# A feed-forward pass in straight-line code: second product in rows, wide sums on DVE, last scaling on ACT

## The chip, the cores and the metric

One core of a Trainium2 chip runs the kernel. The metric is the device time of one execution in microseconds (us). The engines go by short names: PE or TensorE (matrix products; PEld are its weight loads), DVE (VectorE), ACT (ScalarE), POOL (GpSimd) and SP (SyncE, which issues most of the transfers). All numbers are fp32. An fp32 product is two matmul instructions, and the trace counts instructions.

## What is computed

The reference runs a relational graph layer twice, then a transformer block with attention along the edges, on 50,000 nodes of 128 features and 25,000 edges, with a layer norm and a residual around each. The change lies in the end of the transformer block, which treats each node by itself:

```python
x = residual + att                      # att = agg @ Wo + bo
residual = x
h = _layer_norm(x, g2, b2)
ffn = gelu(h @ W1 + bf1) @ W2 + bf2     # 128 -> 512 -> 128
block = residual + ffn
...
x = _layernorm(x + block)               # the kernel's output
```

The kernel has g2 and b2 folded into W1 and bf1. The attention stage leaves two rows per node in the DRAM tensor `x_rows`: X1, the block's input x, and X2, the residual with the attention's output but without `bo`. The output is the layer norm of X1 + X2 + bo + ffn.

## The kernel before

The kernel is a series of programs, one after the other with a barrier between: `prepare`, `dense`, two of `layer`, `attention`, `softmax`, `weighted`, and last `ffn`. The nodes go through `ffn` in 98 groups of 512 (GT = 4 tiles of 128 nodes; a group lies in SBUF as 128 partitions by 4 nodes by 2 by 128 features, 512 KB). Each engine walks the same series of steps, in order, and in step n does its several pieces of work for groups n, n-1, n-2 and so on; semaphores that count groups tie the engines together.

`over_tiles` (line 54) writes the steps: the first 16 as straight code, then a hardware loop (`Fori`) with 16 steps unrolled in its body, then the rest. `Turn.ago(lag)` gives the group that is `lag` steps back. In the loop the semaphore values come from registers. `gate` (line 166) adds an increment of a semaphore of its own ahead of waiting instructions on SP, POOL and DVE.

What a group g goes through, with its lag:

- SP loads both rows of 512 nodes into `xs[g % 16]` (lag 0, line 1671), and stores `res` (lag 14, line 1661).
- POOL adds `bo` to X2 (lag 0, line 1698), adds X2 to X1 (lag 1, line 1705), and computes the inverse roots `rstd` (lag 3) and `rstd2` (lag 12) by two instructions of 4 columns each, `var` (line 1687) and a power of -0.5 (line 1690).
- DVE takes mean and variance of X2 (bn_stats line 1784, bn_aggr line 1798, lag 2), scales it to `normed` (lag 4), adds the second product to X1 (lag 11, line 1778), takes mean and variance of that (lines 1791 and 1810), and scales it to `res` (lag 13). Both scalings are in the helper at line 1769, four instructions of 128 columns.
- PE turns `normed` so that features lie on partitions (lag 5, line 1723, `p_n`), makes the first product in four chunks of 128 hidden features (lag 7, line 1717, `p_f`), the second, summed over the four chunks (lag 8, line 1730, `p_y`), and turns that back into rows of nodes (lag 10, line 1737, `p_r`).
- ACT copies the turned rows to `nT` (lag 6, line 1754), makes the gelus (lag 7, line 1761), and copies the second product with the bias `bf2` per partition to `yT` (lag 9, line 1749).

The second product has the weights stationary and the activations moving, and so comes out with features on partitions:

```python
mm = e.matmul(p_y[:], w_2[:, ch, :], g_T[:, s, ch, :], start=(ch == 0), stop=(ch == FCH - 1))
...
e.activation(yT[:, s, :], p_y[:], ACT.Identity, bias=bf2[:]).then_inc(yT_ready, 1)
...
mm = e.transpose(p_r[s][:, a * D:(a + 1) * D], yT[:, s, a * P:(a + 1) * P], ident[:])
```

## Time and profile before

| | |
|---|---|
| median of 3 executions | 2708.08 us (2704.77 to 2711.64) |
| the profiled execution | 2707.31 us, its span 2705.6 us |
| busy over the span | PE 79%, PEld 57%, DVE 74%, ACT 45%, POOL 61% |
| `ffn` | from the first load's issue at 1910.73 us to the end |
| busy time of the two products of `ffn` | `p_f` 354.1 us, `p_y` 352.8 us |

The shares are means over stages with different limits; only the stretch from 1910 us on bears on the change. Matmuls overlap one another in the trace, so the duration of a group of matmuls says less than the distance between starts. "Idle before" is an engine's waiting time just ahead of an instruction, put down to whatever ended last. POOL's durations are rough.

### The profile page before, as it was taken

The page shows a single profiled execution, that of the slowest core. Times are in us where ns is not written, and L with a number is a line of the kernel's source. Part 1 is how long each engine was busy: PE and PEld are TensorE (multiplying, and loading weights), DVE is VectorE, ACT ScalarE, POOL GpSimd, SP SyncE. Part 2 cuts the span into 40 slices and gives each one's busy share as a digit, 9 for nine tenths or more (in the row PEclk, how much of TensorE's full clock was granted, in tenths as well). Part 3 has the DMA queues.
Part 4 walks back from the last instruction along what each step waited for, and adds up shares of the span by engine and source line. Part 5 has one row for each costly group of instructions (what it writes and reads, how often), then busy time and mean ns, then how long its engine had stood idle before and what let it go on. Part 6 is the DMA issues. An engine that isn't in the chain of part 4 may idle for free. (4 is left out here: it accounts for less than half of the span.)

```text
span 2705.6 us, 46439 instructions
## 1 busy us (share of the span) xinstructions
PE 2142.7 (79%) x11670; PEld 1533.3 (57%) x11670; DVE 1996.6 (74%) x7853; ACT 1204.7 (45%) x2725; POOL 1663.1 (61%) x1791
## 2 busy tenths in 40 slices
PE   3777776747776777599999228885499999999997
PEld 3555555537776777568778226664244444444443
DVE  4888888856665777688888766664467877887775
ACT  2888888832222454456666200000244444444443
POOL 2777777757775776275552007777666666666662
PEclk9889899879888998899999659887799999999999
DMA  3788788766657999644452024664322333333231
GB/s 87 224 244 241 238 240 241 235 186 179 183 165 221 297 300 278 205 127 124 122 126 80 17 71 147 184 194 140 116 78 99 104 105 99 100 105 105 94 98 50
DMA packets 378850, 422.87 MB, mean 156 GB/s; under 512 B 54814, under 2 KB 263274, under 8 KB 378614
## 3 DMA queue, kind: packets, MB, share of 16 engines
q1 hardware_dynamic: 334774, 337.16, 39.9%
q0 software_dynamic: 40768, 82.23, 11.7%
q8 instruction: 84, 1.38, 0.2%
q14 instruction: 152, 1.25, 0.1%
q10 hardware_dynamic: 3072, 0.86, 0.1%
HBM read 273.58 MB, written 179.87 MB: 168 GB/s over the span
## 5 line engine op out<-in xcount | busy, mean ns | idle before, releaser
L1717 PE MATMUL p_f<-nT,w 128*128 128x512 f32 x784 | 354.1, 594 | 0.0
L1730 PE MATMUL p_y<-g_T,w 128*128 128x512 f32 x784 | 352.8, 593 | 0.8 <-ACT yT L1749 0.8
L1120 POOL DMA_INDIRECT x_src<-x_rows,idx x196 | 185.7, 947 | 166.1 <-DVE normed L1287 73.0
L1761 ACT ACTIVATE g_T<-p_f,bf 128x512 f32<-128x512 f32 x392 | 261.5, 688 | 34.6 <-PE p_f L1717 34.4
L1525 POOL DMA_INDIRECT x_rows<-xv,idx x196 | 211.5, 1079 | 85.9 <-issue 52.1
L1698 POOL TENSOR_TENSOR xs<-xs,bo_rows 128x512 f32<-128x512 f32 x98 | 129.0, 1317 | 212.4 <-DMA xs<-x_rows 197.2
L575 POOL DMA_INDIRECT x_dst<-in_x_dram,idx x196 | 195.2, 996 | 101.7 <-issue 101.7
L911 POOL DMA_INDIRECT h_src<-h_table,idx x196 | 191.1, 975 | 87.4 <-issue 56.7
L911 POOL DMA_INDIRECT h_src<-in_x_dram,idx x196 | 190.4, 972 | 75.8 <-issue 58.5
L1690 POOL TENSOR_TENSOR rstd<-var,minus_half 128x4 f32<-128x4 f32 x196 | 206.8, 1055 | 35.9 <-POOL var L1687 35.8
L1749 ACT ACTIVATE yT<-p_y,bf 128x512 f32<-128x512 f32 x98 | 67.4, 688 | 358.9 <-PE p_r L1737 352.5
L579 POOL DMA_INDIRECT e_h<-in_L_gnn_rel_embed_dram,idx x196 | 189.1, 965 | 59.8 <-issue 59.8
L1717 PEld LDWEIGHTS p_f<-nT,w 128*128 128x128 f32 x784 | 142.2, 191 | 142.4 <-issue 119.7
L1730 PEld LDWEIGHTS p_y<-g_T,w 128*128 128x128 f32 x784 | 141.5, 190 | 142.6 <-issue 141.6
L976 ACT ACTIVATE low<-p_h 128x512 f32<-128x512 f32 x98 | 58.5, 597 | 342.9 <-PE p_h L949 342.9
L1754 ACT ACTIVATE nT<-p_n 128x512 f32<-128x512 f32 x98 | 57.7, 589 | 329.9 <-PE p_n L1723 329.9
L1778 DVE TENSOR_TENSOR xs<-p_r,xs 128x512 f32<-128x512 f32 x98 | 67.8, 692 | 181.9 <-PE p_r L1737 181.9
L1769 DVE TENSOR_SCALAR normed<-xs,mv,rstd 128x128 f32<-128x128 f32 x392 | 168.1, 492 | 1.9 <-POOL rstd L1690 1.3
L1769 DVE TENSOR_SCALAR res<-xs,mv,rstd 128x128 f32<-128x128 f32 x392 | 167.4, 488 | 0.8 <-POOL rstd L1690 0.8
L652 PE MATMUL p_r<-ident,h1T 128*128 128x128 f32 x392 | 69.6, 305 | 119.6 <-ACT h_rows L689 119.4
L948 PE MATMUL p_h<-w_r,accT 128*128 128x128 f32 x784 | 160.9, 289 | 0.0
L949 PE MATMUL p_h<-w_sl,ownT 128*128 128x128 f32 x784 | 159.2, 286 | 0.0
(297 smaller groups left out, 5886.8 us busy)
## 6 DMA issues: line engine op xcount, KB each, us to landing
xs<-x_rows SPq DMA_DIRECT2D x98, 512.0 KB, 3.7
x_in<-in_x_dram SPq DMA_DIRECT2D x98, 256.0 KB, 3.7
h_table<-h_rows SPq DMA_DIRECT2D x98, 256.0 KB, 4.0
x_rows<-x_in SPq DMA_DIRECT2D x98, 256.0 KB, 4.5
out_dram<-res SPq DMA_DIRECT2D x98, 256.0 KB, 2.0
x_rows<-x_rows SPq DMA_DIRECT2D x50, 500.0 KB
rows<-edge_rows SPq DMA_DIRECT2D x147, 128.0 KB, 4.5
edge_x<-x_dst SPq DMA_DIRECT2D x98, 128.0 KB
```

The source lines that it names most:

```text
L575: e.indirect_dma_start(out=x_dst[:, m % PN, j, :], out_offset=None, in_=x, in_offset=bass.IndirectOffsetOnAxis(ap=idx[:, DST, 2 * m + j:2 ...
L579: e.indirect_dma_start(out=e_h[:, t, :], out_offset=None, in_=L0_gnn_rel_embed, in_offset=bass.IndirectOffsetOnAxis(ap=idx[:, TYPE, t:t + ...
L911: e.indirect_dma_start(out=h_src[:, g % HN, j, :], out_offset=None, in_=(x, h1_table)[l], in_offset=bass.IndirectOffsetOnAxis(ap=idx[:, (S ...
L948: e.matmul(p_h[g % 2][:, at], accT[:, g % 2, at], w_r[l][:], start=True, stop=False)
L949: mm = e.matmul(p_h[g % 2][:, at], ownT[:, g % 2, at], w_sl[l][:], start=False, stop=True)
L1120: e.indirect_dma_start(out=x_src[:, k % SN, j, :], out_offset=None, in_=x_rows, in_offset=bass.IndirectOffsetOnAxis(ap=idx[:, X_SRC, t:t + ...
L1525: e.indirect_dma_start(out=both_table.rearrange("n a d -> n (a d)"), in_=xv[:, g % VN, j, :, :].rearrange("p a d -> p (a d)"), in_offset=None,
L1690: e.tensor_tensor(rstd[:, s, :], var[:, s, :], minus_half[:], ALU.pow).then_inc(rstd_ready, 1)
L1717: e.matmul(p_f[ch][:], w_1[:, ch * P:(ch + 1) * P], nT[:, s, :], start=True, stop=True)\
L1730: mm = e.matmul(p_y[:], w_2[:, ch, :], g_T[:, s, ch, :], start=(ch == 0), stop=(ch == FCH - 1))
L1761: e.activation(g_T[:, s, ch, :], p_f[ch][:], ACT.Gelu, bias=bf1[:, ch:ch + 1]).then_inc(gelu_ready, 1)
L1769: ins = e.tensor_scalar(into[:, a * D:(a + 1) * D], rows_in[:, a, :], mean[:, a, 0:1], scale[:, a:a + 1], ALU.subtract, ALU.mult)
```

## The change

The change rewrites `ffn` and nothing else, except that `bf2` is now loaded as a row repeated on all 128 partitions (`bf2_rows`).

- All steps are straight code; `Turn`, `over_tiles`, `gate` and their semaphores are gone, and every wait is for a constant.
- The second product has the activations stationary: for each of the four tiles of nodes and each chunk, `g_T` (128 x 128) is the stationary operand and 128 columns of `w_2` move. It comes out in rows of nodes, in one of two PSUM buffers. The copy `yT` and the turn back `p_r` are gone; the PSUM they held is used for a second `p_n` and `p_y`.
- The bias `bf2`, which `yT` added, is now added to X1 in rows by DVE.
- DVE makes all wide sums: X2 + bo, X1 + X2, + bf2, + second product. POOL keeps `var` and the power.
- The last scaling moves from DVE to ACT, four instructions of 128 columns with scale `rstd2` and bias `shift2` = -mean x rstd2, which DVE computes (4 columns). They stand between the gelus.
- `xs` has 14 buffers instead of 16, `res` 4 instead of 16. Lags: DVE's first work 2 steps behind the load, the store 13.

The core of the diff (line 1624 of the new file is the wait before the store, and so on in order):

```diff
-        bf2 = sb("bf2", [P, 1])
+        bf2_rows = sb("bf2_rows", [P, D])
...
-                    e.dma_start(bf2[:], L1_gnn_bf2.rearrange("(p a) -> p a", a=1)).then_inc(loaded, 16)
+                    e.dma_start(bf2_rows[:], L1_gnn_bf2.partition_broadcast(P)).then_inc(loaded, 16)
...
+            XN, RN = 14, 4
...
-                yT = sb("yT", [P, 2, GROUP], F32, c)
...
-                p_n = ps("p_n", c)
...
-                p_y = ps("p_y", c)
-                p_r = [ps(f"p_r{s}", c) for s in range(2)]
...
+                shift2 = sb("shift2", [P, 2, GT], F32, c)
+                p_n = [ps(f"p_n{s}", c) for s in range(2)]
...
+                p_y = [ps(f"p_y{s}", c) for s in range(2)]
...
+                A = 2
+                STEPS = NG + A + 12
...
+                        if at_step(n, A + 11):
+                            g = n - A - 11
+                            if g == NG - 1:
+                                e.wait_ge(stored[(g - 1) % RN], 16 * ((g - 1) // RN + 1))
+                            e.wait_ge(res_ready, g + 1)
+                            e.dma_start(rows(out, g).rearrange("(p a) d -> p (a d)", a=GT), res[:, g % RN, :, :].rearrange("p a d -> p (a d)"))\
+                                .then_inc(stored[g % RN], 16)
+                        if at_step(n, 0):
+                            g = n
+                            wait(e, res_ready, g - XN + 1)
+                            wait(e, both_ready, g - XN + 1)
+                            wait(e, normed_ready, g - XN + 1)
+                            e.dma_start(xs[:, g % XN, :, :, :].rearrange("p a w d -> p (a w d)"),
+                                        rows(both_table, g).rearrange("(p a) w d -> p (a w d)", a=GT)).then_inc(xs_loaded[g % XN], 16)
...
+                    for n in range(STEPS):
+                        if at_step(n, A + 1):
+                            g = n - A - 1
+                            e.wait_ge(mv_ready, g + 1)
+                            e.tensor_scalar(var[:, g % 2, :], mv[:, g % 4, :, 1], EPS, None, ALU.add).then_inc(var_ready, 1)
+                            e.wait_ge(var_ready, g + 1)
+                            wait(e, normed_ready, g - 1)
+                            e.tensor_tensor(rstd[:, g % 2, :], var[:, g % 2, :], minus_half[:], ALU.pow).then_inc(rstd_ready, 1)
+                        if at_step(n, A + 8):
+                            g = n - A - 8
+                            e.wait_ge(mv2_ready, g + 1)
+                            e.tensor_scalar(var2[:, g % 2, :], mv2[:, g % 4, :, 1], EPS, None, ALU.add).then_inc(var2_ready, 1)
+                            e.wait_ge(var2_ready, g + 1)
+                            wait(e, res_ready, g - 1)
+                            e.tensor_tensor(rstd2[:, g % 2, :], var2[:, g % 2, :], minus_half[:], ALU.pow).then_inc(rstd2_ready, 1)
...
+                    for n in range(STEPS):
+                        if at_step(n, A + 5):
+                            g = n - A - 5
+                            e.wait_ge(nT_ready, g + 1)
+                            for ch in range(FCH):
+                                wait(e, gelu_ready, FCH * (g - 1) + ch + 1)
+                                e.matmul(p_f[ch][:], w_1[:, ch * P:(ch + 1) * P], nT[:, g % 2, :], start=True, stop=True).then_inc(f_prod, 1)
+                        if at_step(n, A + 6):
+                            g = n - A - 6
+                            e.wait_ge(gelu_ready, FCH * (g + 1))
+                            wait(e, sum_ready, g - 1)
+                            for a in range(GT):
+                                for ch in range(FCH):
+                                    mm = e.matmul(p_y[g % 2][:, a * D:(a + 1) * D], g_T[:, g % 2, ch, a * P:(a + 1) * P], w_2[:, ch, :],
+                                                  start=(ch == 0), stop=(ch == FCH - 1))
+                            mm.then_inc(y_prod, 1)
+                        if at_step(n, A + 3):
+                            g = n - A - 3
+                            e.wait_ge(normed_ready, g + 1)
+                            wait(e, nT_ready, g - 1)
+                            for a in range(GT):
+                                mm = e.transpose(p_n[g % 2][:, a * P:(a + 1) * P], normed[:, g % 2, a, :], ident[:])
+                            mm.then_inc(n_turned, 1)
...
-                            e.activation(yT[:, s, :], p_y[:], ACT.Identity, bias=bf2[:]).then_inc(yT_ready, 1)
...
+                    for n in range(STEPS):
+                        if at_step(n, A + 4):
+                            g = n - A - 4
+                            e.wait_ge(n_turned, g + 1)
+                            wait(e, f_prod, FCH * (g - 1))
+                            e.activation(nT[:, g % 2, :], p_n[g % 2][:], ACT.Copy).then_inc(nT_ready, 1)
+                        for ch in range(FCH):
+                            if at_step(n, A + 5):
+                                g = n - A - 5
+                                e.wait_ge(f_prod, FCH * g + ch + 1)
+                                if ch == 0:
+                                    wait(e, y_prod, g - 1)
+                                e.activation(g_T[:, g % 2, ch, :], p_f[ch][:], ACT.Gelu, bias=bf1[:, ch:ch + 1]).then_inc(gelu_ready, 1)
+                            if at_step(n, A + 10):
+                                g = n - A - 10
+                                if ch == 0:
+                                    e.wait_ge(shift2_ready, g + 1)
+                                    wait(e, stored[g % RN], 16 * (g // RN))
+                                ins = e.activation(res[:, g % RN, ch, :], xs[:, g % XN, ch, X1, :], ACT.Identity,
+                                                   scale=rstd2[:, g % 2, ch:ch + 1], bias=shift2[:, g % 2, ch:ch + 1])
+                                if ch == GT - 1:
+                                    ins.then_inc(res_ready, 1)
...
+                    for n in range(STEPS):
+                        if at_step(n, A + 7):
+                            g = n - A - 7
+                            x1 = xs[:, g % XN, :, X1, :]
+                            e.wait_ge(y_prod, g + 1)
+                            e.wait_ge(both_ready, g + 1)
+                            e.tensor_tensor(x1, p_y[g % 2][:].rearrange("p (a d) -> p a d", a=GT), x1, ALU.add).then_inc(sum_ready, 1)
+                        if at_step(n, A):
+                            g = n - A
+                            x2 = xs[:, g % XN, :, X2, :]
+                            e.wait_ge(xs_loaded[g % XN], 16 * (g // XN + 1))
+                            e.tensor_tensor(x2, x2, over_rows(bo_rows), ALU.add).then_inc(x2_ready, 1)
+                        if at_step(n, A + 7):
+                            g = n - A - 7
+                            e.wait_ge(sum_ready, g + 1)
+                            wait(e, mv2_ready, g - 1)
+                            for a in range(GT):
+                                ins = e.bn_stats(stats2[:, g % 2, a, :], xs[:, g % XN, a, X1, :])
+                            ins.then_inc(stats2_ready, 1)
...
+                        if at_step(n, A + 2):
+                            g = n - A - 2
+                            e.wait_ge(rstd_ready, g + 1)
+                            wait(e, n_turned, g - 1)
+                            for a in range(GT):
+                                ins = e.tensor_scalar(normed[:, g % 2, a, :], xs[:, g % XN, a, X2, :], mv[:, g % 4, a, 0:1],
+                                                      rstd[:, g % 2, a:a + 1], ALU.subtract, ALU.mult)
+                            ins.then_inc(normed_ready, 1)
+                        if at_step(n, A + 9):
+                            g = n - A - 9
+                            e.wait_ge(rstd2_ready, g + 1)
+                            wait(e, res_ready, g - 1)
+                            e.scalar_tensor_tensor(out=shift2[:, g % 2, :], in0=mv2[:, g % 4, :, 0], scalar=-1.0, in1=rstd2[:, g % 2, :],
+                                                   op0=ALU.mult, op1=ALU.mult).then_inc(shift2_ready, 1)
...
+                        if at_step(n, A + 3):
+                            g = n - A - 3
+                            x1 = xs[:, g % XN, :, X1, :]
+                            e.tensor_tensor(x1, x1, xs[:, g % XN, :, X2, :], ALU.add).then_inc(pair_ready, 1)
+                        if at_step(n, A + 4):
+                            g = n - A - 4
+                            x1 = xs[:, g % XN, :, X1, :]
+                            e.wait_ge(pair_ready, g + 1)
+                            e.tensor_tensor(x1, x1, over_rows(bf2_rows), ALU.add).then_inc(both_ready, 1)
```

On PE, one step of the middle of the pass and the start of the next, before. `p_f` is the first product, `p_n` the turn of the normed rows, `p_y` the second product, `p_r` the turn back.

```order
L1717 MATMUL p_f_1<-nT,w_1 128x512 x4
L1723 MATMUL p_n<-ident,normed 128x128 x4
L1730 MATMUL p_y<-g_T,w_1 128x512 x4
L1737 MATMUL p_r_1<-ident,yT 128x128 x4
L1717 MATMUL p_f_1<-nT,w_1 128x512 x4
```

And now:

```order
L1663 MATMUL p_f_1<-nT,w_1 128x512 x4
L1670 MATMUL p_y_1<-w_1,g_T 128x128 x16
L1678 MATMUL p_n_1<-ident,normed 128x128 x4
L1663 MATMUL p_f_1<-nT,w_1 128x512 x4
L1670 MATMUL p_y_1<-w_1,g_T 128x128 x16
```

The second product has four times as many instructions of a quarter of the columns and stands right behind the first; the turn back is gone. An x16 there is 32 matmul instructions in the trace.

On DVE, one step before (`stats` and `mv` belong to the first norm, `stats_1`, `mv_1` and `rstd_1` to the second):

```order
L1778 TENSOR_TENSOR xs<-p_r_1,xs 128x4x128
L1781 REGISTER_ALU
L1784 BN_STATS stats<-xs 128x6 x4
L1791 BN_STATS stats_1<-xs 128x6 x4
L1798 BN_AGGR mv<-stats 128x2 x4
L1769 TENSOR_SCALAR normed<-xs,mv,rstd 128x128 x4
L1810 BN_AGGR mv_1<-stats_1 128x2 x4
L1769 TENSOR_SCALAR res<-xs,mv_1,rstd_1 128x128 x4
```

And now:

```order
L1717 TENSOR_TENSOR xs<-p_y_1,xs 128x4x128
L1722 TENSOR_TENSOR xs<-xs,bo_rows 128x4x128
L1728 BN_STATS stats_1<-xs 128x6 x4
L1735 BN_STATS stats<-xs 128x6 x4
L1742 BN_AGGR mv_1<-stats_1 128x2 x4
L1749 TENSOR_SCALAR normed<-xs,mv,rstd 128x128 x4
L1756 SCALAR_TENSOR_TENSOR shift_1<-mv_1,rstd_1 128x4
L1763 BN_AGGR mv<-stats 128x2 x4
L1768 TENSOR_TENSOR xs<-xs 128x4x128
L1773 TENSOR_TENSOR xs<-xs,bf_rows 128x4x128
```

The scaling to `res` has left; three wide sums and the small shift have come, and work for different groups alternates, so that most waits of DVE for its own results have another piece between.

## Rows read from the trace of the kernel before

**Rows 1.** Windows: stretch; busy us of PE, PEld, DVE, ACT, POOL; clock; DMA.
```profile
2200.00:2300.00 100.00, 100.00 (x312) 49.40 (x311) 80.32 (x323) 47.82 (x78) 65.78 (x78) 1.00 0.31 100
```

**Rows 2.** Chain that ended last, 2594 to 2613: start us, us, what.
```profile
2596.94 3.44 PE p_y L1730 x8
2600.38 0.44 PE p_r L1737 x4
2600.82 3.44 PE p_f L1717 x8
2604.25 0.44 PE p_n L1723 x4
```

**Rows 3.** Waits, 2000 to 2600: who waited for whom, us, times, longest.
```profile
ACT yT L1749 <- PE p_r L1737: 282.9, 77, 3.7
```

**Rows 4.** Timeline of TensorE in a graph layer: start us, us, what.
```profile
912.92 0.39 PE L948 MATMUL p_h<-w_r,accT 128*128 128x128 f32 x2
...
914.49 0.39 PE L949 MATMUL p_h<-w_sl,ownT 128*128 128x128 f32 x2
```

**Rows 5.** Line 948, its weight loads: ns min/median/max.
```profile
L948 PEld LDWEIGHTS p_h<-w_r,accT x784: 190/192/337, 584.1 to 1124.5; 128*128 128x128 f32 x196
```

**Rows 6.** Timeline of DVE in the middle of the pass.
```profile
2205.86 0.69 DVE L1778 TENSOR_TENSOR xs<-p_r,xs 128x512 f32<-128x512 f32 x1 [0.85 <-PE p_r L1737]
2206.47 0.86 DVE L1784 BATCH_NORM_STATS2 stats<-xs 128x6 f32<-128x128 f32 x4
2207.24 0.85 DVE L1791 BATCH_NORM_STATS2 stats<-xs 128x6 f32<-128x128 f32 x4
2208.02 0.36 DVE L1798 BATCH_NORM_AGGREGATE mv<-stats 128x2 f32<-128x6 f32 x4
```

**Rows 7.** Timeline, end of the pass.
```profile
2685.97 3.70 PE L1730 MATMUL p_y<-g_T,w 128*128 128x512 f32 x8 [0.84 <-ACT yT L1749]
...
2692.19 1.08 DVE L1769 TENSOR_SCALAR res<-xs,mv,rstd 128x128 f32<-128x128 f32 x4
2693.20 0.68 DVE L1778 TENSOR_TENSOR xs<-p_r,xs 128x512 f32<-128x512 f32 x1
...
2693.91 0.87 DVE L1791 BATCH_NORM_STATS2 stats<-xs 128x6 f32<-128x128 f32 x4
...
2701.14 1.11 DVE L1769 TENSOR_SCALAR res<-xs,mv,rstd 128x128 f32<-128x128 f32 x4 [0.75 <-POOL rstd L1690]
```

**Rows 8.** Timeline of POOL and DVE, middle of the pass.
```profile
2202.23 0.23 POOL L1687 TENSOR_SCALAR var<-mv 128x4 f32<-128x4 f32 x1
...
2202.64 1.04 POOL L1690 TENSOR_TENSOR rstd<-var,minus_half 128x4 f32<-128x4 f32 x1 [0.18 <-POOL var L1687]
...
2202.81 0.57 DVE L1769 TENSOR_SCALAR res<-xs,mv,rstd 128x128 f32<-128x128 f32 x2
...
2203.55 1.45 DVE L1769 TENSOR_SCALAR res<-xs,mv,rstd 128x128 f32<-128x128 f32 x1
...
2203.65 1.27 POOL L1705 TENSOR_TENSOR xs<-xs 128x512 f32<-128x512 f32 x1
```

**Rows 9.** Groups by line and form, whole span: busy us, mean ns, idle before.
```profile
L709 ACT ACTIVATE x_in<-x_in,shift,rstd 128x128 f32<-128x128 f32 x294 | 123.6, 483 | 3.1
...
L764 DVE TENSOR_TENSOR x_in<-h,x_in 128x512 f32<-128x512 f32 x98 | 67.0, 684 | 0.0
...
L759 DVE SCALAR_TENSOR_TENSOR shift<-mv,rstd 128x4 f32<-128x4 f32 x98 | 14.4, 147 | 0.1
```

**Rows 10.** Timeline, start of the pass.
```profile
1910.73 8.89 SPq L1671 DMA_DIRECT2D xs<-x_rows  x14
1914.48 2.55 POOL L1698 TENSOR_TENSOR xs<-xs,bo_rows 128x512 f32<-128x512 f32 x2 [15.43 <-DMA xs<-x_rows]
...
1922.18 3.02 DVE L1769 TENSOR_SCALAR normed<-xs,mv,rstd 128x128 f32<-128x128 f32 x4 [1.27 <-POOL rstd L1690]
...
1930.12 5.07 PE L1717 MATMUL p_f<-nT,w 128*128 128x512 f32 x8
```

208 lines of the change are left out of this document (36 added, 172 removed).

## The prediction

> **What bounds the kernel now.** I read the windows first: the reader should see TensorE busy for 100.00 of 100 us in the middle of the feed-forward pass at a granted clock of 1.00 (the 2.4 GHz level), with DVE at 80.32 and ACT at 47.82 [rows 1]. Busy alone proves little, so the chain of waits comes next. From 2596.94 to 2604.69 (2604.25 + 0.44) it is one unbroken TensorE string: second product 3.44, turn back 0.44, first product 3.44, turn of the normed rows 0.44 [rows 2]. That is one group in 7.75 us, and 98 groups make 759 of the span's 2705.6 us. The table of waits says the same from the other side: ACT waits for the turn back 282.9 us in 600 [rows 3], and DVE is idle a fifth of the time. So in this pass a microsecond off DVE, ACT or POOL is worth nothing by itself, one off TensorE is worth 98 times itself until another engine takes over. Everything ahead of the pass (to 1910.73 us) is untouched but for one small load of the bias, 64 KB where it was 512 bytes, ahead of others of the same kind; I price it at nothing (the ends are 0 and 3.7 us, the landing of a far larger load [rows 10]).
>
> **TensorE, per group.** Removed: the turn back, 4 transposes, 0.44 us [rows 2]. Changed: the second product. It was 8 matmul instructions with 512 columns (two per fp32 product), 3.44 us. Now it is 16 products of 128 columns, 32 instructions with a weight load each; the columns in total are the same. Its nearest rows are the products of the graph layers, also fp32, 128x128, stationary operand changed every time and accumulated: eight of them start 0.224 us apart in pairs of instructions (912.92 to 914.49 is seven steps, 1.57 us) at an undisturbed clock [rows 4]. 16 x 0.224 = 3.59 us, so +0.15 us. The lower end is no cost (3.44, if only columns counted).
> The row first: in these pairs the weight loads take 0.19 us each by the profile [rows 5], yet a pair of matmuls keeps starting every 0.224 us, so the loads lie beneath the streams. The Trainium skill ("TensorE: Matmul & The Clock Gate", Part 3, What overlaps and what doesn't) says that a weight load overlaps matmuls in flight only when it goes to other rows of the array. By that rule the 32 loads would stand in the open; the row decides against it, and it is a rival below.
> New period: 7.75 - 0.44 + 0.15 = 7.46 us.
>
> **DVE, per group.** Costs by the distance to the next start, since instructions overlap by some 80 ns. The final sum 0.61 (2205.86 to 2206.47), four bn_stats 0.77 twice, four bn_aggr 0.28 twice (0.36 less that overlap) [rows 6]; four scalings 1.01 when POOL is quiet (2692.19 to 2693.20) [rows 7]. Before, with both scalings: 0.61 + 1.54 + 0.56 + 2.02 = 4.73, and the rest of its 6.2 us of busy time per group (0.8032 x 7.75) is blocking by POOL's two wide sums. A single scaling lasted 1.45 us there beneath POOL's 1.27 us sum, where a free one takes about 0.3 [rows 8].
> After: the scaling to `res` goes (-1.01). Three wide sums come, all with both inputs in SBUF; such sums stand in the first stage with a mean of 684 ns [rows 9], next to 692 for the present one, so 3 x 0.61 = 1.83. A shift of 4 columns comes, 0.15 [rows 9]. Total 2.44 + 1.54 + 0.56 + 1.01 + 0.15 = 5.70 us, 1.76 below TensorE's 7.46. Its waits on its own results have at least one other group of instructions between them.
> **Does POOL still block it?** What POOL keeps is two `var` (0.23) and two `pow` (1.04) per group. The trace answers for the scaling: `pow` ran from 2202.64 to 2203.68, and inside it two scalings that began at 2202.81 were done in 0.57 together, at their free pace; the stall came only with the wide sum of 2203.65 [rows 8]. So a four-column `pow` holds nothing for its 1.04 us. For a wide sum with two SBUF inputs beside a `pow` there is no row: the ends are 0 and the whole 2 x (0.23 + 1.04) = 2.54 us. I take 0, the value of the nearest row.
>
> **ACT, per group.** Before 0.69 + 0.59 + 4 x 0.69 = 4.04. Now `yT` goes (-0.69) and four scalings of 128 columns with scale and bias per row come; those of the first stages have a mean of 483 ns [rows 9], which is the upper end in a row, since neighbours overlap: 1.9. Sum about 5.3 us (4.04 - 0.69 + 1.93). They stand between the gelus, which then come every 1.2 us while TensorE makes a chunk every 0.86; the last gelu of a group ends some 2 us after its chunk, and its product starts a step later. Hidden by 2 us; if ACT were to pass 7.46 us, the second product's wait for `gelu_ready` would be late first.
>
> **POOL and SP.** POOL falls to 2.54 us per group. `rstd2` now also waits for the group two earlier to be stored into `res` by ACT, with a whole step of slack. SP waits for `res_ready` of group n-13, then loads group n, which DVE wants two steps later: some 15 us for a landing of 3.75 us (1910.73 to 1914.48 [rows 10]). What queues behind DVE's new wait for the load is everything DVE does, the final sum excepted, but that load has the slack just named; before, POOL asked for it in the same step. Fourteen buffers for sixteen change nothing then.
>
> **Start of the pass.** The first load lands by 1914.48. Then POOL's wide sums and DVE's scalings get in each other's way: the first four scalings take 3.02 us, and the first product starts at 1930.12 [rows 10]. After: steps of x2 + stats + aggr, with nothing between to cover the waits, 2.05 us each (sum to stats 0.71, by [rows 7]; stats 0.87, and I put 0.15 for the wait on it; aggr 0.3), so two of them reach 1918.6; then scaling of group 0 to 1921.1 (0.71 + 0.78 + 1.01), aggr 0.3, the same again for group 1 to 1923.9; its turn 0.9 (TensorE is below full speed there: the first product takes 5.07 us, not 3.44 [rows 10]), first product at 1924.8. Gain about 5.2 us. Loads keep up: after the first, POOL's second sum followed without a wait [rows 10].
>
> **End of the pass.** Now 15.9 us pass from the last product's end (2689.67) to 2705.6, since three groups still queue on DVE with `res` among them [rows 7]. After: sum, stats, aggr 2.4 us; the scalings of the groups 95, 96 and 97 on ACT follow at 1.9 us each, the first at 2.5, so the last row is there at 8.2 (`pow` of group 97, which waits for 95 to be scaled at 4.4, is ready by 5.6, ahead of its turn), and the present 3.4 us from last row (2702.25) to end [rows 7] make 11.6 us. Gain 4.3 us. TensorE's one stall of 0.84 us there, waiting for `yT` [rows 7], goes too.
>
> **Sum.** 98 x 0.15 = +14.7; 96 turns back x 0.44 = -42.2 (the last two lie in the tail); stall -0.8; start -5.2; end -4.3. Together -37.8 us. The profiled execution took 2707.31 us (0.8 us below the median of three, 2708.08): 2707.3 - 37.8 = 2669.5 us, so **2669 us**.
>
> **The rivals.**
> 1. *DVE becomes the bound* (slower). Mechanism: POOL's `pow` and `var` read SBUF while DVE's new sums read two inputs from it, and one waits the other out. The place is the three sums beside the two `pow` of a group. At the full 2.54 us DVE needs 5.70 + 2.54 = 8.24 us per group, 0.78 over TensorE: 2669 + 98 x 0.78 = 2745 us. It decides from 1.76 us of blocking per group and turns the result slower from 2.15 us. Against it: the scalings inside a `pow` did not slow [rows 8]; and the `pow` falls after bn_aggr, partly into DVE's idle time. The Trainium skill ("SBUF — State Buffer", Who interferes with whom) has this rule: a DVE instruction with two SBUF inputs contends with a GpSimd instruction that reads SBUF, and the later one waits for all of the other. 6%.
> 2. *The weight loads are not hidden* in the second product. If each of the 32 instructions took the 0.19 us of its load rather than 0.11, it would be 6.1 us for 3.59: 2669 + 98 x 2.5 = 2914 us. Against it: [rows 4]. By the page's rule named above. 1%.
> 3. *Only columns count*: second product 3.44 us, 98 x 0.15 less, 2654 us. 6%.
> 4. *The period comes as forecast, the ends do not* (fill bound by loads, tail by the store): 2679 us. 10%.
> 5. *The turn back was no cost*, because something else sets 7.75 us per group: then only start, end and stall, 10.3 us, are left: 2697 us. For it, ACT and DVE with their new work could have a chain of waits that I do not see; against it, the unbroken string [rows 2]. 5%.
> The forecast itself has 72%, with 2660 to 2678 as its own range (0.04 us of period either way is 4 us; fill and tail 3 us, and executions shown differ by 3 us to either side). Over 0.3% (8 us, what can be told from no change here): faster 0.92, same 0.02, slower 0.06, the last two from rivals 1 and 2 and part of their way there. The range that leaves out rivals 1 and 2 and the margin of 5 is 2654 to 2690 us.
>
> **What would show it.** In the new profile: TensorE still at 10 tenths and clock 1.00 through the pass; starts of the first product 7.46 us apart; the 16 products of a group 3.59 us; wide sums on DVE at about 690 ns, none near 1.7 us; DVE busy near 5.9 us of 7.46; ACT 5 to 5.4; first product 14 us after the first load is issued, where it was 19.4; about 12 us from last product to end. I am wrong if DVE waits nowhere for `y_prod` and TensorE waits for `sum_ready` or `normed_ready` (rival 1), or if the 128-column pace is not 0.112 us per instruction (rivals 2 and 3).

## The result, and the profile after the change

| | before | after |
|---|---|---|
| median | 2707.94 us (4 executions, 2704.77 to 2711.64) | 2665.51 us (4 executions, 2662.84 to 2666.21) |
| the profiled execution | 2707.31 us, span 2705.6 | 2666.12 us, span 2664.4 |
| from the first load's issue of `ffn` to the end of the span | 794.9 us | 754.3 us |

The ratio is 0.9835 (95% interval 0.9823 to 0.9847): 42.4 us less by the medians, 41.2 by the profiled executions. The forecast was 2669 us, in a range of 2654 to 2690.

Windows of the kernel after, 2200 to 2300: stretch; busy us of PE, PEld, DVE, ACT, POOL; clock; DMA.

```profile
2200.00:2300.00 100.00, 100.00 (x597) 74.65 (x597) 76.28 (x338) 61.21 (x122) 35.05 (x53) 1.00 0.32 104
```

TensorE is busy throughout at a granted clock of 1.00, as in [rows 1]; DVE's share has fallen from 80.32 to 76.28 and POOL's from 65.78 to 35.05, ACT's has risen from 47.82 to 61.21. The chain that ended last, in the middle of the pass (start us, us, what):

```profile
2598.90 0.44 PE p_n L1678 x4
2599.34 3.44 PE p_f L1663 x8
2602.77 3.57 PE p_y L1670 x32
```

This answers to [rows 2]. The string is still TensorE alone, and a period is 0.44 + 3.44 + 3.57 = 7.45 us; the median distance between second products is 7.443 us, where it was 7.745. The turn back is gone, and the second product costs 0.13 us more. The waits, 2000 to 2600 us (who for whom, us, times, longest):

```profile
POOL rstd L1653 <- ACT res L1701: 383.2, 81, 5.0
ACT nT L1688 <- PE p_n L1678: 214.0, 81, 2.6
DVE xs L1717 <- PE p_y L1670: 144.2, 81, 1.8
```

ACT and DVE wait for TensorE; the one large wait of POOL, ahead of its second root, is for ACT's scaling (383.2 us), and no row of the table has an engine waiting for POOL. The middle of the pass in the timeline:

```profile
2200.22 0.68 ACT L1695 ACTIVATE g_T<-p_f,bf 128x512 f32<-128x512 f32 x1
...
2200.79 0.49 ACT L1701 ACTIVATE res<-xs,shift,rstd 128x128 f32<-128x128 f32 x1
...
2201.17 0.68 ACT L1695 ACTIVATE g_T<-p_f,bf 128x512 f32<-128x512 f32 x1
...
2204.44 0.69 DVE L1717 TENSOR_TENSOR xs<-p_y,xs 128x512 f32<-128x512 f32 x1 [1.77 <-PE p_y L1670]
...
2205.05 0.68 DVE L1722 TENSOR_TENSOR xs<-xs,bo_rows 128x512 f32<-128x512 f32 x1
...
2205.65 0.86 DVE L1728 BATCH_NORM_STATS2 stats<-xs 128x6 f32<-128x128 f32 x4
...
2206.43 0.85 DVE L1735 BATCH_NORM_STATS2 stats<-xs 128x6 f32<-128x128 f32 x4
...
2207.21 0.36 DVE L1742 BATCH_NORM_AGGREGATE mv<-stats 128x2 f32<-128x6 f32 x4
...
2207.48 1.08 DVE L1749 TENSOR_SCALAR normed<-xs,mv,rstd 128x128 f32<-128x128 f32 x4
```

Four things stand here. DVE waits 1.77 us for the second product in each group, and then runs through the sum (0.61 to the next start), the first of the three new sums (0.60), the eight bn_stats and so on. The new sums are at their free duration: over the whole pass, the line of X2 + bo gives (ns min/median/max)

```profile
L1722 DVE TENSOR_TENSOR xs<-xs,bo_rows x98: 658/681/701, 1913.6 to 2607.0; 128x512 f32<-128x512 f32 x98
```

and the other two 654/660/683 and 680/685/693. The four scalings to `normed` take 1.08 us, where POOL's sums had stretched scalings before [rows 8]. And two gelus with one scaling of ACT between them start 0.95 us apart, not 1.2. The start of the pass, to be read beside [rows 10]:

```profile
1910.04 6.21 SPq L1632 DMA_DIRECT2D xs<-x_rows  x13
1913.61 0.69 DVE L1722 TENSOR_TENSOR xs<-xs,bo_rows 128x512 f32<-128x512 f32 x1 [42.74 <-DMA xs<-x_rows]
...
1918.92 1.10 DVE L1749 TENSOR_SCALAR normed<-xs,mv,rstd 128x128 f32<-128x128 f32 x4
...
1923.01 0.66 DVE L1768 TENSOR_TENSOR xs<-xs 128x512 f32<-128x512 f32 x1
1923.18 0.57 POOL L1643 TENSOR_SCALAR var<-mv 128x4 f32<-128x4 f32 x1 [1.09 <-DVE mv L1763]
...
1923.59 0.68 DVE L1722 TENSOR_TENSOR xs<-xs,bo_rows 128x512 f32<-128x512 f32 x1
1923.77 5.24 PE L1663 MATMUL p_f<-nT,w 128*128 128x512 f32 x8
1923.84 1.33 POOL L1646 TENSOR_TENSOR rstd<-var,minus_half 128x4 f32<-128x4 f32 x1
```

The first four scalings take 1.10 us where they took 3.02, and the first product starts 13.73 us behind the first load's issue where that was 19.38. The end, beside [rows 7]:

```profile
2654.18 0.69 DVE L1717 TENSOR_TENSOR xs<-p_y,xs 128x512 f32<-128x512 f32 x1 [1.51 <-PE p_y L1670]
...
2656.27 4.72 ACT L1701 ACTIVATE res<-xs,shift,rstd 128x128 f32<-128x128 f32 x12 [1.92 <-DVE shift L1756]
```

The last twelve scalings follow one another in 4.72 us (0.39 each), and 3.4 us later the kernel ends. From the product's end to the kernel's end it is 10.4 us; before it was 16.1. Here and in the table below the product ends one pace behind the start of its last matmul instruction (0.11 us, before 0.43); by the end that the profile records for that instruction (2654.14, before 2689.67), which the prediction used, it is 10.2 and 15.9, and the gain is the same 5.7.

Where the 41.2 us went: 5.7 at the start, 29.2 between the first product's start and the last second product's end, 5.7 at the end, and 0.7 ahead of the pass.

### The profile page after: what moved, and what is told of

The parts are those of the page before. It is cut to its first block and busy times, and to the rows that moved or that the text cites. A ratio compares the mean times of both kernels' runs of the same rounds, so it can differ in the third digit from the quotient of the medians.

```text
span 2664.4 us, 47955 instructions
## 1 busy us (share of the span) xinstructions
PE 2108.4 (79%) x13630; PEld 1693.7 (64%) x13630; DVE 1957.4 (73%) x7853; ACT 1283.9 (48%) x3019; POOL 1426.5 (54%) x1595
## 5 line engine op out<-in xcount | busy, mean ns | idle before, releaser
L1670 PEld LDWEIGHTS p_y<-w,g_T 128*128 128x128 f32 x3136 | 365.4, 192 | 46.4 <-issue 24.2
L1670 PE MATMUL p_y<-w,g_T 128*128 128x128 f32 x3136 | 365.8, 275 | 0.0
L1653 POOL TENSOR_TENSOR rstd<-var,minus_half 128x4 f32<-128x4 f32 x98 | 113.5, 1159 | 450.3 <-ACT res L1701 450.2
L1695 ACT ACTIVATE g_T<-p_f,bf 128x512 f32<-128x512 f32 x392 | 267.1, 681 | 31.4 <-PE p_f L1663 31.3
L1717 DVE TENSOR_TENSOR xs<-p_y,xs 128x512 f32<-128x512 f32 x98 | 67.8, 692 | 184.8 <-PE p_y L1670 184.8
L1701 ACT ACTIVATE res<-xs,shift,rstd 128x128 f32<-128x128 f32 x392 | 189.3, 487 | 4.7 <-DVE shift L1756 4.7
L608 PEld LDWEIGHTS p<-w_el,h1T 128*128 128x128 f32 x784 | 107.6, 203 | 71.9 <-DVE h1T L756 41.1
L1011 DVE TENSOR_SCALAR mate<-rows,seg_col,norm_col 128x128 f32<-128x128 uint8 x392 | 141.1, 363 | 10.2 <-DMA rows<-edge_rows 10.0
L1002 DVE SCALAR_TENSOR_TENSOR accT<-rows,accT,p_acc 128x128 f32<-128x128 uint8 x390 | 132.2, 339 | 12.6 <-PE p_acc L892 7.5
```

Of the source, the lines that this page charges most:

```text
L1011: ins = e.tensor_scalar(mate[:, g % 2, j * P:(j + 1) * P], row_of(g, j, SEG), seg_col[:, t:t + 1], norm_col[:, t:t + 1], ALU.is_equal, ALU ...
L1670: mm = e.matmul(p_y[g % 2][:, a * D:(a + 1) * D], g_T[:, g % 2, ch, a * P:(a + 1) * P], w_2[:, ch, :], start=(ch == 0), stop=(ch == FCH - 1))
L1695: e.activation(g_T[:, g % 2, ch, :], p_f[ch][:], ACT.Gelu, bias=bf1[:, ch:ch + 1]).then_inc(gelu_ready, 1)
L1701: ins = e.activation(res[:, g % RN, ch, :], xs[:, g % XN, ch, X1, :], ACT.Identity, scale=rstd2[:, g % 2, ch:ch + 1], bias=shift2[:, g % 2 ...
```

## The experiments

They ran on four chips, and there every kernel takes 440 to 510 us longer ahead of the pass than in the two executions above (the kernel before, timed beside them, 460 to 500 us longer as a whole); why is not shown. In the stretch from 100 to 500 us the transfers move 155 GB/s in the changed kernel, where the profile above has 240, and the first load of `ffn` is issued at 2347 to 2415 us instead of 1910. So the whole time is about 3170 to 3210 us before, most executions of one kernel lie within 1% of their median, and a ratio tells little of 8 us. The pass itself is the same there as far as it was measured: the unchanged code of `ffn`, only unrolled, takes 795.8 us there against 794.9 above, the changed one 754.5 against 754.3. I therefore read each experiment by its pass in the profile, and divide it by four points in time: first load's issue, first product's start, last second product's end, end of the span.

| kernel | start | middle | end | pass, us | period | ratio to before, 95% |
|---|---|---|---|---|---|---|
| before | 19.4 | 759.4 | 16.1 | 794.9 | 7.745 | |
| the change | 13.7 | 730.2 | 10.4 | 754.3 | 7.443 | 0.9835, 0.9823 to 0.9847 |
| changed_again | 13.7 | 730.4 | 10.4 | 754.5 | 7.443 | 0.984, 0.978 to 0.991 |
| unroll_only | 19.3 | 760.0 | 16.5 | 795.8 | 7.745 | 0.999, 0.995 to 1.002 |
| rows_only | 23.0 | 731.0 | 9.6 | 763.6 | 7.446 | 0.989, 0.984 to 0.993 |
| columns_again | 13.8 | 758.7 | 14.8 | 787.3 | 7.742 | 0.994, 0.991 to 0.997 |
| sums_on_pool | 21.3 | 731.0 | 10.4 | 762.7 | 7.443 | 0.984, 0.978 to 0.991 |
| scaling_on_dve | 13.7 | 730.2 | 9.2 | 753.1 | 7.443 | 0.981, 0.973 to 0.990 |
| four_more_powers | 15.4 | 730.1 | 10.4 | 755.8 | 7.443 | 0.986, 0.981 to 0.992 |
| two_more_wide_sums | 15.7 | 729.5 | 10.4 | 755.6 | 7.443 | 0.988, 0.984 to 0.991 |
| second_product_bf16 | 13.7 | 538.3 | 10.9 | 562.9 | 5.572 | 0.924, 0.916 to 0.931 |
| bf16_bias_on_pool | 14.8 | 574.6 | 10.9 | 600.3 | 5.974 | 0.939, 0.933 to 0.945 |
| both_products_bf16 | 13.6 | 539.1 | 10.4 | 563.1 | 5.571 | 0.927, 0.919 to 0.936 |
| bf16_bias_on_pe | 13.7 | 510.3 | 11.0 | 535.1 | 5.196 | 0.914, 0.909 to 0.920 |

### unroll_only: the straight code alone

The kernel before, with its loop written out.

```diff
-    for n in range(peeled * unroll):
-        step(Turn(n, n % unroll, n // unroll, total, unroll))
-    with eng.Fori(peeled, total // unroll) as b:
-        for k in range(unroll):
-            step(Turn(b * unroll + k, k, b, total, unroll))
-    for n in range(total // unroll * unroll, total + lag):
+    for n in range(total + lag):
```

> The kernel before with all its steps as straight code and nothing else changed. Theory (TensorE's own instructions set the period of a group; code form and the other engines show only at the start and the end of the pass): no change, 2707 us within 3, p_y starts 7.745 us apart. Rival (register instructions between the matmuls of the loop, and on the other engines, cost time, and straight code is part of the gain): period below 7.7 us, 5 to 15 us faster.

The pass took 795.8 us, 0.9 more than before and no less. The chain that ended last, in the middle of the pass:

```profile
2700.02 3.44 PE p_y L1724 x8
2703.46 0.44 PE p_r L1731 x4
2703.90 3.44 PE p_f L1711 x8
2707.33 0.44 PE p_n L1717 x4
```

It is the string of [rows 2] to 0.01 us. TensorE never waits in the middle, so whatever the registers and gates of the loop cost an engine there, they cost it beside TensorE. The rival that straight code is part of the gain fell.

### rows_only: the product in rows in the old loop

The kernel before, its loop and its scalings on DVE kept; `yT` and `p_r` gone, and the bias as a third wide sum on POOL.

```diff
-                            for ch in range(FCH):
-                                e.wait_ge(gelu_ready, FCH * g.n + ch + 1)
-                                mm = e.matmul(p_y[:], w_2[:, ch, :], g_T[:, s, ch, :], start=(ch == 0), stop=(ch == FCH - 1))
...
+                            e.wait_ge(gelu_ready, FCH * g.n + FCH)
...
+                                for ch in range(FCH):
+                                    mm = e.matmul(p_y[s][:, a * D:(a + 1) * D], g_T[:, s, ch, a * P:(a + 1) * P], w_2[:, ch, :],
+                                                  start=(ch == 0), stop=(ch == FCH - 1))
```

> The kernel before, its hardware loop kept, with the second product in rows alone; the bias bf2 becomes a third wide sum on POOL, the last scaling stays on DVE. Theory: period 7.44 us (7.745 - 0.435 + 0.13), so 98 x 0.30 = 29 us less, another 1 to 4 us less at the end (no yT, no turn back, lags shorter by two), up to 2 us more at the start for POOL's third sum: about 2677 us. DVE 5.9 to 7.2 us busy of 7.44 with more blocking, hidden. Rival (the relief of POOL was needed for it): POOL needs 3 x 1.27 + 2.54 = 6.35 us, blocks DVE for up to 3.8 us per group, DVE becomes the bound at up to 8.5 us: 2700 to 2780 us.

```profile
2701.04 3.57 PE p_y L1733 x32
2704.61 3.44 PE p_f L1719 x8
2708.05 0.44 PE p_n L1725 x4
```

The period is the changed kernel's, 7.446 us, with POOL's wide sums still there. The middle is 28.4 us shorter than before, and the end 6.5, where I had expected 1 to 4: two steps less follow the product. The start is 3.7 us longer, and there my bound of 2 was too small:

```profile
2407.34 7.70 SPq L1668 DMA_DIRECT2D xs<-x_rows  x12
...
2420.32 3.98 DVE L1761 TENSOR_SCALAR normed<-xs,mv,rstd 128x128 f32<-128x128 f32 x4 [2.49 <-POOL rstd L1687]
...
2430.36 1.92 PE L1719 MATMUL p_f<-nT,w 128*128 128x512 f32 x2
```

The first four scalings take 3.98 us beside three wide sums of POOL (3.02 beside two [rows 10]). The product in rows by itself gives 31.3 us of the 40.5 that the pass lost.

### columns_again: the change without the product in rows

The changed kernel with the second product in 512 columns, `yT` (without bias) and the turn back. With them come back two steps of lag, 16 buffers of `xs`, and one `p_n` and one `p_y` where the change has two of each.

```diff
-                            for a in range(GT):
-                                for ch in range(FCH):
-                                    mm = e.matmul(p_y[g % 2][:, a * D:(a + 1) * D], g_T[:, g % 2, ch, a * P:(a + 1) * P], w_2[:, ch, :],
-                                                  start=(ch == 0), stop=(ch == FCH - 1))
...
+                            for ch in range(FCH):
+                                mm = e.matmul(p_y[:], w_2[:, ch, :], g_T[:, g % 2, ch, :], start=(ch == 0), stop=(ch == FCH - 1))
```

> The changed kernel with only the second product back in the old form (512 moving columns, yT on ACT, turn back on TensorE, two steps more of lag). Theory: period 7.74 us, 29 us more in the middle, 2 to 4 us more at the end: 2697 to 2700 us; ACT at 5.9 us per group is hidden. Rival (the gain came from DVE, POOL and the straight code): period stays near 7.44, below 2680 us.

```profile
2701.74 3.43 PE p_y L1673 x8
2705.17 0.44 PE p_n L1680 x4
2705.61 0.44 PE p_r L1687 x4
2706.05 3.44 PE p_f L1667 x8
```

The whole string has come back to the period before, 7.742 us. The pass is 33.0 us longer than the changed one: 28.5 in the middle, 4.4 at the end, nothing at the start. So every other edit together, without this one, gives 7.6 us: 5.6 at the start, 0.7 in the middle and 1.3 at the end.

### sums_on_pool: the wide sums back on POOL

X2 + bo, X1 + X2 and + bf2 by POOL, the rest as in the change.

```diff
+                        if at_step(n, A - 1):
...
+                            e.tensor_tensor(x2, x2, over_rows(bo_rows), ALU.add).then_inc(x2_ready, 1)
+                        if at_step(n, A):
...
+                            e.tensor_tensor(x1, x1, xs[:, g % XN, :, X2, :], ALU.add).then_inc(pair_ready, 1)
+                        if at_step(n, A + 2):
...
+                            e.tensor_tensor(x1, x1, over_rows(bf2_rows), ALU.add).then_inc(both_ready, 1)
```

> The changed kernel with the three wide sums without a product (X2 + bo, X1 + X2, + bf2) on POOL. Theory: period stays 7.44 us, first product again 17 to 20 us after the first load's issue instead of 13.7, end unchanged: 2669 to 2673 us; DVE's busy time per group falls from 5.68 us by 1.83 and grows by blocking of its normed scaling, at most 3.8. Rival (moving the sums off POOL bought part of the period): period above 7.5 us, 2675 us or more.

Windows, 2700 to 2800:

```profile
2700.00:2800.00 100.00, 100.00 (x603) 75.13 (x602) 51.76 (x287) 60.02 (x120) 83.60 (x94) 1.00 0.33 107
```

The middle moved by 0.8 us only, with POOL at 83.60 and DVE at 51.76, where the change has 35 and 76. The start did: 21.3 us, 7.6 more than the change, and more than I had expected. So the three sums on POOL cost 8.3 us of the pass, nearly all at its start, and not in the throughput, where one would suspect it. This kernel has one wide sum more on POOL than the kernel before, the bias.

### scaling_on_dve: the last scaling back on DVE

```diff
-                                ins = e.activation(res[:, g % RN, ch, :], xs[:, g % XN, ch, X1, :], ACT.Identity,
-                                                   scale=rstd2[:, g % 2, ch:ch + 1], bias=shift2[:, g % 2, ch:ch + 1])
...
-                            e.scalar_tensor_tensor(out=shift2[:, g % 2, :], in0=mv2[:, g % 4, :, 0], scalar=-1.0, in1=rstd2[:, g % 2, :],
-                                                   op0=ALU.mult, op1=ALU.mult).then_inc(shift2_ready, 1)
...
+                            for a in range(GT):
+                                ins = e.tensor_scalar(res[:, g % RN, a, :], xs[:, g % XN, a, X1, :], mv2[:, g % 4, a, 0:1],
+                                                      rstd2[:, g % 2, a:a + 1], ALU.subtract, ALU.mult)
```

> The changed kernel with the last scaling back on DVE (four tensor_scalar of 128 columns to res, no shift2). Theory (cover): DVE needs 5.68 - 0.09 + 1.00 = 6.6 us per group, still under TensorE's 7.44, so the period stays 7.44 us and the pass (first load's issue to end) is within 2 us of the changed kernel's 754.3. Rival (moving the scaling off DVE was needed): the period rises above 7.5 us, the pass to 760 us or more.

```profile
2700.00:2800.00 100.00, 100.00 (x604) 75.13 (x603) 88.42 (x374) 43.57 (x66) 44.63 (x55) 1.00 0.33 107
```

DVE is at 88.42, or 6.58 us per group, still beneath 7.44. Nothing moves in the middle, and the end is 1.2 us shorter (9.2 for 10.4), since DVE's four scalings take 1.08 us and ACT's 1.57 (4.72 / 3). The move to ACT costs 1.2 us of the gain here; that it pays where DVE is the bound was not run.

### four_more_powers and two_more_wide_sums: what POOL does to DVE

The changed kernel, with work on POOL whose results nobody uses.

```diff
+                            for k in range(4):
+                                e.tensor_tensor(spare[:, k, :], twos[:], minus_half[:], ALU.pow)
```

> The changed kernel with four more powers of 4 columns per group on POOL, into a tile nobody reads, so that POOL is busy for 6.8 of 7.44 us with them. Theory (a power holds nothing that DVE's sums need for its 1.04 us): no wide sum on DVE above 0.75 us, period 7.44 us, pass 754 to 757 us. Rival (the port rule to the letter: the later of two waits the other out): wide sums on DVE of up to 1.7 us, DVE at 7 to 8.7 us per group, period 7.5 to 8.7 us, pass up to 870 us.

Timeline of POOL and DVE, 2702 to 2704:

```profile
2702.36 1.04 POOL L1651 TENSOR_TENSOR rstd<-var,minus_half 128x4 f32<-128x4 f32 x1
2702.48 0.66 DVE L1776 TENSOR_TENSOR xs<-xs 128x512 f32<-128x512 f32 x1
2703.05 0.69 DVE L1781 TENSOR_TENSOR xs<-xs,bf_rows 128x512 f32<-128x512 f32 x1
```

Two sums with both inputs in SBUF start beneath one power and take 0.66 and 0.69 us; the longest of all 294 new sums took 693 ns. So not even three times the number of powers stretches a sum on DVE. DVE does wait for what POOL makes, since the useful powers now come later. Waits, 2650 to 2850:

```profile
DVE shift L1764 <- POOL rstd L1661: 39.3, 27, 1.5
```

That wait takes the place of the one for the second product and is hidden in the middle. At the start it is not: the second group's `var` begins only behind four spare powers, DVE's scaling waits 1.47 us for that root, and the start is 1.6 us longer.

```diff
+                            for k in range(2):
+                                e.tensor_tensor(spare[:, k, :, :], bo_rows[:].unsqueeze(1).to_broadcast([P, GT, D]),
+                                                bf2_rows[:].unsqueeze(1).to_broadcast([P, GT, D]), ALU.add)
```

> The changed kernel with two more wide sums of two SBUF rows per group on POOL, into a tile nobody reads. Theory (wide sums on POOL and on DVE with two SBUF inputs exclude each other): some of DVE's wide sums last 1.2 to 2.0 us, where 0.68 is free, and DVE needs 1 to 2.6 us more per group: period 7.44 (if its 1.77 us of slack holds it) to 8.3 us. Rival (only the scaling on DVE is ever blocked): DVE's wide sums stay at 0.66 to 0.70 us, period 7.44.

Timeline of POOL and DVE, 2698.5 to 2702, and then the line of DVE's sum X2 + bo:

```profile
2697.22 2.85 POOL L1650 TENSOR_TENSOR spare<-bo_rows,bf_rows 128x512 f32<-128x512 f32 x2
...
2699.46 1.47 DVE L1754 TENSOR_SCALAR normed<-xs,mv,rstd 128x128 f32<-128x128 f32 x4
```

```profile
L1727 DVE TENSOR_TENSOR xs<-xs,bo_rows x98: 653/681/1809, 2382.0 to 3076.6; 128x512 f32<-128x512 f32 x98
```

Wide sums do hold DVE: the four scalings take 1.47 us for 1.08, their mean is 426 ns (2650 to 2850 us) where the free one is 336, and single sums reach 1.81 us. But the median of the sums stayed free (681 ns), since only 6 of the 294 took over 0.75 us, and the period did not move: DVE has 1.76 us to spare.

### The bf16 runs: how much cover DVE leaves

With the string shortened, DVE's 5.70 us should show itself as the bound. Second product in bf16 (`g_T` and `w_2` rounded to it):

```diff
-                g_T = sb("g_T", [P, 2, FCH, GROUP], F32, c)
+                g_T = sb("g_T", [P, 2, FCH, GROUP], BF16, c)
+                w_2h = sb("w_2h", [P, FCH, D], BF16, c)
...
+                    e.activation(w_2h[:], w_2[:], ACT.Copy).then_inc(w_2h_ready, 1)
```

> The changed kernel with gelu's output and w_2 in bf16 for the second product: one matmul instruction for two, a quarter of the streaming. Theory: TensorE falls to 3.44 + 0.44 + 0.9 to 1.8 = 4.8 to 5.7 us per group, and DVE (5.68 us) becomes the bound, with ACT at 5.2 close behind: period 5.7 to 6.0 us, 140 to 170 us faster than the changed kernel, pass 585 to 615 us. Rival (some chain of waits across the engines stands just beneath 7.44 us): period 6.5 us or more.

```profile
2700.00:2800.00 100.00, 91.58 (x505) 47.28 (x503) 100.00 (x451) 79.34 (x163) 59.61 (x73) 1.00 0.43 143
```

TensorE now waits (91.58 of 100) and DVE never does (100.00): the period is 5.572 us, which is DVE's own work per group, put at 5.70 in the prediction. Both the period and the pass (562.9 us) came out under what I had expected for this run (5.7 to 6.0, 585 to 615). The first product in bf16 too:

```diff
-                nT = sb("nT", [P, 2, GROUP], F32, c)
...
+                nT = sb("nT", [P, 2, GROUP], BF16, c)
+                w_1h = sb("w_1h", [D, FFN], BF16, c)
```

> As second_product_bf16, with nT and w_1 in bf16 too, so that TensorE needs about 2.3 us per group. Theory (DVE alone sets the period now): period 5.57 us, no change in the middle of the pass, 1 to 5 us less at its start. Rival (TensorE and its waits still count): period below 5.4 us.

```profile
2700.00:2800.00 100.00, 68.67 (x425) 41.78 (x426) 100.00 (x451) 79.56 (x162) 69.07 (x73) 0.77 0.43 142
```

The period is the same to 0.001 us, so a lighter TensorE is worth nothing there. Its granted clock was 0.77 in this stretch, a mean over pieces at 1.2 and at 2.4 GHz, and the engine was busy for 68.67 of 100 us; in the run above it was busy for 91.58 at a clock of 1.00. The start did not get shorter by the 1 to 5 us I had expected, only by 0.1.

Then one wide sum off DVE, in two ways. To POOL:

```diff
+                        if at_step(n, A):
...
+                            e.tensor_tensor(x1, x1, bf2_rows[:].unsqueeze(1).to_broadcast([P, GT, D]), ALU.add).then_inc(pair_ready, 1)
```

> The kernel with the second product in bf16, whose bound is DVE at 5.57 us per group, with the sum X1 + bf2 moved back to POOL as soon as the load lands. Theory (a wide sum on POOL takes DVE's instructions with two SBUF inputs and its scaling out for as long as it runs, but little else): DVE needs 5.57 - 0.61 = 4.96 us plus 0 to 1.27 of blocking, so the period is 5.0 to 5.6 us if POOL's sum falls beside bn_stats at least in part, pass 505 to 565 us. Rival (the blocking gives back all and more, as in the kernel before): period above 5.6 us.

```profile
2705.07 2.08 DVE L1759 TENSOR_SCALAR normed<-xs,mv,rstd 128x128 f32<-128x128 f32 x4
...
2705.81 1.25 POOL L1646 TENSOR_TENSOR xs<-xs,bf_rows 128x512 f32<-128x512 f32 x1
```

This was a miss: I had expected a period of 5.0 to 5.6 us and it became 5.97, as the rival had it. DVE lost a sum of 0.61 us and got 1.0 us of blocking for it: the four scalings take 2.08 us with POOL's sum inside them, where they take 1.08 by themselves. And onto TensorE, as a product of a row of ones with the bias that starts the accumulation (bf16 as well):

```diff
+                            e.matmul(p_y[g % 2][:], ones_h[:], bf2_h[:].rearrange("p a d -> p (a d)"), start=True, stop=False)
...
-                                    mm = e.matmul(p_y[g % 2][:, a * D:(a + 1) * D], g_T[:, g % 2, ch, a * P:(a + 1) * P], w_2[:, ch, :],
-                                                  start=(ch == 0), stop=(ch == FCH - 1))
+                                    mm = e.matmul(p_y[g % 2][:, a * D:(a + 1) * D], g_T[:, g % 2, ch, a * P:(a + 1) * P], w_2h[:, ch, :],
+                                                  start=False, stop=(a == GT - 1 and ch == FCH - 1))
```

> As second_product_bf16, with bf2 added by TensorE (one bf16 product of a row of ones with the bias, 512 columns, ahead of the sixteen) instead of by DVE. Theory (DVE's instructions alone set 5.57 us): DVE falls to 5.57 - 0.61 = 4.96 us, TensorE rises to 3.44 + 0.44 + 0.9 + 0.2 = 5.0 us, so both stand at the bound: period 5.0 to 5.2 us, pass 510 to 530 us, some 40 to 50 us less than second_product_bf16 in its pass of 563. Rival (with two engines equally loaded, waits between them add up): period 5.3 us or more.

Windows, 2650 to 2800 (150 us):

```profile
2650.00:2800.00 150.00, 150.00 (x841) 80.37 (x841) 146.07 (x693) 130.98 (x261) 72.41 (x116) 1.00 0.46 152
```

The period is 5.196 us, TensorE busy for 150.00 of 150 us at a clock of 1.00, DVE for 146.07. The pass of 535.1 us is 5 over the upper end that I had given (530), the period at its upper end (5.2), and the step from second_product_bf16 is less than the 40 to 50 us expected. It is the fastest of all here, 2904.5 us against 3171.7 us of the kernel before on the same chip, with a pass 27.8 us shorter than second_product_bf16's. What it leaves out is precision: the second product's operands and the bias are rounded to bf16.

changed_again is the changed kernel with no edit, for the comparison between chips.

> The changed kernel once more, on the chip of this series, as the standard for the two below. Expected: pass 754 us as in its first profile, period 7.443 us, about 40 us less than the kernel before whatever the stages ahead of the pass take on this chip.

It took 3134.94 us against 3177.72 us, 42.8 us less (by the interval, 30 to 71), where the first executions gave 42.4; that the whole times agree so well is luck. The pass agrees to 0.2 us, so it takes the same time however fast the stages ahead of it are.

## Why the prediction was right

The parts by undoing one at a time: product in rows 33.0 us, sums off POOL 8.3, scaling to ACT -1.2; and the straight code by itself 0 (-0.9 as measured, which two profiles cannot tell from nothing). Together 40.1 of the 40.5 us that the pass lost. The match is closer than the parts allow: the 8.3 us are against three wide sums on POOL, and the kernel before had two.

- **TensorE's term** held. The second product was forecast at +0.15 us from the pace of the graph layer [rows 4] and took +0.13; the period was to be 7.46 and is 7.44. By the two ends (3.44 if only columns counted, 3.59) it stands at the upper one, so rival 3 fell: 32 instructions of 128 columns are 4% dearer than 8 of 512. The middle was to lose 28.3 us (14.7 - 42.2 - 0.8) and lost 29.2.
- **The weight loads** (rival 2) are hidden. In the kernel after, the weight loads of the line of the second product read (ns min/median/max, then first and last):

```profile
L1670 PEld LDWEIGHTS p_y<-w,g_T x3136: 190/192/192, 1932.3 to 2653.8; 128*128 128x128 f32 x196
```

  They take 0.192 us each, as in [rows 5], 6.1 us in a group, and yet the 32 instructions take 3.57 us, 0.112 each; the loads overlap the matmuls and one another. By the rule of the Trainium skill that the prediction named ("TensorE: Matmul & The Clock Gate", Part 3, What overlaps and what doesn't) they could not overlap the matmuls, since every load goes to all rows; this case's measurement decides against that rule as it stands. The same part of the page also lets a load go ahead when it is to the background weight buffer, which would fit; no run here shows which way the loads take.
- **DVE's 5.70 us** were 5.68 by its busy time (0.7628 x 7.443), and 5.57 where it is the bound. The bf16 run confirms the term best, since nothing covers it there.
- **Rival 1** (DVE blocked by POOL's `var` and power) fell, and four_more_powers is the run that shows it: no sum is held, with three times the powers (DVE's waits there are for POOL's results). That a power holds nothing was taken from DVE's scalings with one SBUF input, and it holds for sums with two as well. The Trainium skill's rule ("SBUF — State Buffer", Who interferes with whom) holds in part: a wide sum of POOL does hold DVE's sums (up to 1.81 us for 0.68 in two_more_wide_sums), but its four-column powers do not; it is they that last longer, as the last section shows.
- **ACT's 5.3 us** was mis-sized: busy for 0.6121 x 7.443 = 4.56. A scaling was priced at its mean duration of 483 ns [rows 9] and a gelu at 0.69 us; neighbours overlap, and in the timeline above a scaling adds 0.38 and a gelu 0.57. ACT lies off the string, so nothing came of it in the middle.
- **The start** was to gain 5.2 and gained 5.7. The cause as forecast is shown: with the sums back on POOL, the start is 7.6 us longer again. That this is 2 us more than the gain goes with the third wide sum (the bias) on POOL, which the kernel before did not have; in rows_only it lengthened the start by 3.7 us.
- **The end** was to gain 4.3 and gained 5.7. The scalings of the last three groups were put at 1.9 us each, 5.7; all twelve took 4.72. This is the same mis-sized term as ACT's, and it makes 1.0 of the 1.4 us. Taking `res` off DVE, which the prediction counted with this gain, is no part of it: with the scaling back on DVE the end is 1.2 us shorter still. What shortened the end is above all the product in rows with its two steps less (4.4 us by columns_again), so the size of this term was in part luck.
- **The stall** of 0.84 us for `yT` is gone, and no other took its place. Rivals 4 (the ends stay) and 5 (the turn back was no cost) fell: both ends moved by 5.7 us, and columns_again loses 33.0 us as soon as the old product and its turn back return.

The sum was -37.8 us against -41.2: 0.9 in the middle, 0.5 at the start, 1.4 at the end and 0.7 ahead of the pass, which I had priced at nothing and which is within what executions differ.

## What to carry to other kernels

When one engine is busy without a gap, look for its work that only changes a layout: choosing which operand is stationary can make the product come out as the next step wants it, and 16 small products cost hardly more than 4 wide ones (3.57 us for 3.44) while four transposes and a copy go. Work taken off an engine that was not the bound paid only at the start of the pass here (7.6 us of 8.3 for the wide sums), through the way POOL held DVE up; the last scaling, moved off DVE, paid nothing and cost 1.2 us at the end. How much cover is left can be measured: shorten the bound until something else sets the period, and if that other engine is then never idle, the period (5.57 us here) is its work.

## What the runs showed of the hardware that I had not expected

- **POOL's wide sums hold DVE's sums, its four-column powers do not**, though the powers last nearly as long (1.04 us for 1.27). Beneath a power DVE's sums keep their 0.66 to 0.69 us (four_more_powers). Whether the width decides or the operation was not tested. The reverse is not free: in the start of the pass above, POOL's `var` takes 0.57 us (0.23 by itself [rows 8]) beside DVE's sum of 1923.01, and its power 1.33 beside that of 1923.59. In the whole pass the 87 powers for `rstd2` that start while one of DVE's sums of two SBUF inputs runs take 1168 to 1189 ns, the other 11 take 1036 to 1037. A wide sum of POOL (1.25 us) holds DVE's scalings too, which read one input from SBUF, as [rows 8] had shown: for 1.0 us of 2.08 in bf16_bias_on_pool.
- **Moving an add from DVE to POOL cost DVE more than making it**: 0.61 us saved, 1.0 us of blocking (bf16_bias_on_pool). As one more matmul instruction at the head of the accumulation the same add made the period 0.38 us shorter (5.57 to 5.20), and DVE was no longer the bound.
- **TensorE's granted clock was 0.77** in the stretch in which it was busy for 69 of 100 us behind DVE (both_products_bf16), and 1.00 where it was busy for 92 (second_product_bf16). Part of the work taken from TensorE was so given back by its clock, and the period, set by DVE, did not change.
